# Ternary weights quantised by ScalarE in chunks during the first attention, in place of a stage of their own

## What is computed

```
x = x + _L0_xattn_ref(_layernorm(x), ctx_2048, Wq, Wkv, Wout, bout)
x = x + _L0_ffn_ref(_layernorm(x), w_gate, w_up, w_down)
...
def weight_quant(w):
    scale = 1.0 / jnp.clip(jnp.mean(jnp.abs(w)), EPS)
    return jnp.clip(jnp.round(w * scale), -1.0, 1.0) / scale
def bitlinear(x, w):
    return jnp.einsum('bsh,oh->bso', act_quant(x), weight_quant(w))
```

## Time and profile before

| | us |
|---|---|
| median of 3 runs | 2633.72 (2631.86 to 2634.31) |
| the profiled execution | 2634.14 |
| its span, first to last instruction | 2632.3 |
| mean granted clock of TensorE | 0.901 of full speed |

### The profile page before, as it was taken

One profiled execution on the slowest core, in us unless ns is written; L12 is line 12 of the kernel. 1 busy time (PEld: TensorE's weight loads), 2 busy tenths in 40 slices (PEclk: granted clock), 3 DMA queues, 4 the chain that ended last, 5 costly groups with the idle time before them and its releaser, 6 DMA issues. The chain is left out here.

```text
span 2632.3 us, 35153 instructions
## 1 busy us (share of the span) xinstructions
PE 2052.2 (78%) x11638; PEld 758.9 (29%) x11670; DVE 1586.2 (60%) x2348; ACT 1160.3 (44%) x1639; POOL 1314.3 (50%) x885
## 2 busy tenths in 40 slices
PE   4999999999999116999858898888944109999980
PEld 1222222222222002444322222222213105555540
DVE  5555555555553577776557777777725805565657
ACT  3555555555554014554324666666643004444420
POOL 2667666666767003766432222222212756777750
PEclk8999999999999558999978999999975559999995
DMA  2001010010101535000013323222201026666647
GB/s 93 22 22 34 22 30 27 29 30 22 34 18 34 200 104 168 1 1 1 0 43 53 59 58 58 54 55 52 45 29 48 1 59 174 202 188 209 193 129 320
DMA packets 166277, 192.37 MB, mean 73 GB/s; under 512 B 51014, under 2 KB 123206, under 8 KB 162928
## 3 DMA queue, kind: packets, MB, share of 16 engines
q1 hardware_dynamic: 143008, 151.38, 20.8%
q0 software_dynamic: 17408, 33.67, 3.9%
q10 hardware_dynamic: 5712, 5.45, 0.6%
HBM read 146.97 MB, written 59.93 MB: 79 GB/s over the span
## 5 line engine op out<-in xcount | busy, mean ns | idle before, releaser
L588 DVE TENSOR_REDUCE a_negmax<-a_ps_max 128x2 f32<-128x1024 f32 x256 | 312.1, 1219 | 226.7 <-PE a_ps_max L429 226.7
L1061 DVE TENSOR_REDUCE a_negmax<-a_ps_max 128x1 f32<-128x512 f32 x512 | 333.2, 683 | 119.5 <-PE a_ps_max L909 116.3
L1008 ACT ACTIVATE a_probs<-a_ps_st 128x512 f32<-128x512 f32 x512 | 288.9, 596 | 197.6 <-PE a_ps_st L930 195.2
L542 ACT ACTIVATE a_probs<-a_ps_st 128x1024 f32<-128x1024 f32 x256 | 262.0, 1024 | 232.2 <-PE a_ps_st L449 232.2
L389 POOL TENSOR_TENSOR a_added_up<-a_added_up,a_probs 128x1024 f32<-128x1024 f32 x128 | 301.0, 2352 | 29.8 <-ACT a_probs L542 27.2
L460 PE MATMUL a_ps_o<-a_probs,a_values 128*64 128x512 f32 x1024 | 276.2, 618 | 0.0
L389 POOL TENSOR_TENSOR a_added_up<-a_probs 128x1024 f32<-128x1024 f32 x64 | 150.2, 2347 | 227.8 <-ACT a_probs L542 227.8
L909 PE MATMUL a_ps_max<-a_k_st,a_q_st 96*128 96x512 f16 x512 | 201.6, 395 | 9.8 <-DVE a_negmax L1061 6.8
L930 PE MATMUL a_ps_st<-a_q_st,a_k_st 97*128 97x512 f16 x512 | 196.7, 386 | 8.3 <-ACT a_probs L1008 2.5
L43 PE MATMUL s_gu<-s_xT,s_gu_h 128*128 128x384 f16 x768 | 189.2, 329 | 1.9 <-DVE s_xT L2177 1.9
L581 DVE SCALAR_TENSOR_TENSOR a_qk_l<-a_ps_misc,a_qk_h 128x512 f16<-128x512 f32 x122 | 84.3, 691 | 137.3 <-ACT a_qk_h L525 137.3
(11 more groups left out here) (414 smaller groups left out, 4261.9 us busy)
## 6 DMA issues: line engine op xcount, KB each, us to landing
s_raw<-in_guT SPq DMA_DIRECT2D x32, 768.0 KB, 5.7
a_inverse<-a_dram_inverse SPq DMA_DIRECT2D x128, 128.0 KB, 3.0
m_y_tok<-f_nothing SPq DMA_DIRECT2D x16, 1024.0 KB, 10.3
c_yg<-m_y_tok SPq DMA_DIRECT2D x16, 1024.0 KB, 7.8
a_ctx_in<-in_ctx SPq DMA_DIRECT2D x32, 256.0 KB, 3.0
s_raw<-in_dnT SPq DMA_DIRECT2D x32, 256.0 KB, 6.0
s_raw<-in_dnT SPq DMA_DIRECT2D x64, 128.0 KB, 6.8
a_q_st<-a_dram_halves SPq DMA_DIRECT2D x48, 128.0 KB, 3.7
```

The source lines that it names most:

```text
L542: act.activation(probs[:, s % RING, :, :], ps_st[:, :, :], ACT.Exp).then_inc(exped, 1)
L588: dve.tensor_reduce(negmax[:, v % 2, :, i % KD], ps_max[:, :, :], AX.X, ALU.max, negate=True).then_inc(maxed, 1)
L1008: act.activation(probs[:, s // HG % 3, s % HG, :], ps_st[:, s % 2, :], ACT.Exp, scale=DH1 ** -0.5).then_inc(exped, 1)
L1061: dve.tensor_reduce(negmax[:, g % 2, at:at + 1], ps_max[:, i % 2, :], AX.X, ALU.max, negate=True).then_inc(maxed, 1)
```

## The change

The quantisation stage is removed. `wq` and `means` become tensors of the whole kernel's first half, and the weights go through 96 chunk turns of the first attention, each 128x512 f32 (256 KB). There are 48 chunks, 16 for each weight, and each is loaded twice.

- First pass, chunks m = 0 to 47 in the even steps 16 to 110: ACT takes the absolute value with a sum over the row into `w_part` (the values it writes into `wq` are overwritten in the second pass).
- At step 114 DVE sums `w_part`; PE multiplies with ones at the end of step 118; at the end of step 119 PE waits for DVE, which makes means and reciprocals.
- Second pass, m = 48 to 95 in the even steps 128 to 222: ACT scales the chunk and adds 12582912, which rounds it, in place; in the odd step after it, it takes the sign of the chunk minus 12582912 and writes the ternary weight into `wq`.
- SP loads each chunk six steps ahead of its turn. There are three slots; the load of m waits until chunk m - 3 has been used, which the first pass signals with its one instruction and the second with the sign.
- The probabilities have 5 buffers for 6, the sums 3 pairs for 4, and queries and keys 7 pairs of heads for 8. The waits that guard these buffers are changed to match. Two constants are set by DVE before the attention, and `ones` has 128 columns for 32.

The rest of the kernel is as before. The diff, cut to its core:

```diff
-def first_attention(nc, x_all, stats, mv, rstd, d):
+def first_attention(nc, x_all, stats, mv, rstd, wq, means, d):
...
-    RING = 6
+    RING = 5
+    CHUNKS = 3 * KD * FF // D
+    PER = CHUNKS // 3
+    SLOTS = 3
+    UPS = 3
+    QK = 7
+    SUMMED_FROM, ROUNDED_FROM = STEPS, 8 * STEPS
+    MEANS_AT = 7 * STEPS + 2
...
-        ones = sb("ones", [P, P // HG], F32)
-        qk_h, qk_l = sb("qk_h", [P, 2, 2 * KD, D], F16), sb("qk_l", [P, 2, 2 * KD, D], F16)
+        ones = sb("ones", [P, P], F32)
+        magic = sb("magic", [P, 2], F32)
+        w_raw = sb("w_raw", [P, SLOTS, D], F32)
+        w_part = sb("w_part", [P, CHUNKS], F32)
+        w_sums = sb("w_sums", [P, 3], F32)
+        w_inv = sb("w_inv", [P, 3], F32)
+        qk_h, qk_l = sb("qk_h", [P, QK, 2, D], F16), sb("qk_l", [P, QK, 2, D], F16)
...
-        added_up = sb("added_up", [P, 2, HG, D], F32)
+        added_up = sb("added_up", [P, UPS, 2, D], F32)
...
+        def chunk_at(s):
+
+            if SUMMED_FROM <= s < SUMMED_FROM + 2 * CHUNKS and s % 2 == 0:
+                return (s - SUMMED_FROM) // 2
+            if ROUNDED_FROM <= s < ROUNDED_FROM + 2 * CHUNKS and s % 2 == 0:
+                return CHUNKS + (s - ROUNDED_FROM) // 2
+            return None
...
+            def load_chunk(m):
+                need(sp, w_used, m - SLOTS + 1)
+                w, c = m % CHUNKS // PER, m % PER
+                src = d[("wgT", "wuT", "wdT")[w]]
+                cols = src.shape[1] // D
+                sp.dma_start(w_raw[:, m % SLOTS, :], src[P * (c // cols):P * (c // cols) + P, D * (c % cols):D * (c % cols) + D]).then_inc(w_in[m % SLOTS], 16)
+
             load_context(1)
             place_maxima(0)
             load_context(2)
             for s in range(T):
                 g = s // 8 - 1
+                if chunk_at(s + 6) is not None:
+                    load_chunk(chunk_at(s + 6))
                 if s % KD == 2 and s // KD + 1 < KD * B:
                     place_maxima(s // KD + 1)
...
+            def total_weights():
+                pe.wait_ge(w_step, 1)
+                pe.wait_ge(maxrow, MEANS_AT // KD + 3)
+                need(pe, sums_kept, MEANS_AT // 8)
+                nc.tensor.matmul(ps_tr[:, 0:3], ones[:, :], w_sums[:, :], start=True, stop=True).then_inc(w_total, 1)
...
+                if s == MEANS_AT + 4:
+                    total_weights()
+                if s == MEANS_AT + 5:
+                    pe.wait_ge(w_step, 3)
...
+            def chunk(m):
+                w, c = m % CHUNKS // PER, m % PER
+                raw_w, out_w = w_raw[:, m % SLOTS, :], wq[:, w, D * c:D * c + D]
+                act.wait_ge(w_in[m % SLOTS], 16 * (m // SLOTS + 1))
+                if m < CHUNKS:
+                    act.activation(out_w, raw_w, ACT.Abs, accum_out=w_part[:, m:m + 1]).then_inc(w_used, 1)
+                else:
+                    act.wait_ge(w_step, 3)
+                    act.activation(raw_w, raw_w, ACT.Identity, bias=magic[:, 0:1], scale=w_inv[:, w:w + 1]).then_inc(w_rounded, 1)
+
+            def chunk_sign(m):
+                w, c = m % CHUNKS // PER, m % PER
+                act.wait_ge(w_rounded, m - CHUNKS + 1)
+                act.activation(wq[:, w, D * c:D * c + D], w_raw[:, m % SLOTS, :], ACT.Sign, bias=magic[:, 1:2], scale=1.0).then_inc(w_used, 1)
...
+                if chunk_at(s) is not None:
+                    chunk(chunk_at(s))
+                if s > ROUNDED_FROM and chunk_at(s - 1) is not None:
+                    chunk_sign(chunk_at(s - 1))
...
+            def weight_sums():
+                dve.wait_ge(w_used, CHUNKS)
+                dve.tensor_reduce(w_sums[:, :], w_part[:, :].rearrange("p (w c) -> p w c", w=3), AX.X, ALU.add).then_inc(w_step, 1)
+
+            def weight_means():
+                dve.wait_ge(w_total, 1)
+                dve.tensor_scalar(means[:, :], ps_tr[:, 0:3], 1.0 / (D * FF), Q_EPS, ALU.mult, ALU.max).then_inc(w_step, 1)
+                dve.wait_ge(w_step, 2)
+                dve.reciprocal(w_inv[:, :], means[:, :]).then_inc(w_step, 1)
...
+                if s == MEANS_AT:
+                    weight_sums()
+                if s == MEANS_AT + 5:
+                    weight_means()
...
-def quantise_weights(nc, wq, means, d):
...
-def ternary_ffn(nc, x_all, stats, mv, rstd, ident, d, y_tok):
+def ternary_ffn(nc, x_all, stats, mv, rstd, wq, means, ident, d, y_tok):
...
-        wq = sb("wq", [P, 3, KD * FF], BF16)
-        means = sb("means", [P, 3], F32)
-        quantise_weights(nc, wq, means, d)
```

More of the change, by code:

```diff
@@ L293, in first_attention @@
                  "weighted kept added summed sums_kept sums_out compact_in recip inverse_out inverse_in normalised out_proj residual").split())
+        w_in = [sem(f"w_in{q}") for q in range(SLOTS)]
+        w_used, w_rounded, w_step, w_total = (sem(n) for n in ("w_used", "w_rounded", "w_step", "w_total"))
         def first_context(sp):
@@ L302, in first_attention @@
             first_context,
-            [(row[:, :, :].bitcast(U32), 0, 0), (shift[:, :], WS, 0)], [(ones[:, :], 1.0, 0)], stats, mv, rstd[:, :, 0], (d["x"], x_all))
+            [(row[:, :, :].bitcast(U32), 0, 0), (shift[:, :], WS, 0)], [(ones[:, :], 1.0, 0), (magic[:, 0:1], MAGIC, 0), (magic[:, 1:2], -MAGIC, 0)], stats, mv, rstd[:, :, 0], (d["x"], x_all))
         block = ctx.enter_context(nc.Block())
@@ L312, in tile_left, with chunk_used_at @@
             need(eng, v_out, KD * n + max(t - 7, 0))
+        def chunk_used_at(m):
+            return SUMMED_FROM + 2 * m if m < CHUNKS else ROUNDED_FROM + 2 * (m - CHUNKS)
+        def chunk_at(s):
[4 more added lines that the diff above has]
+            return None
         def added_by(s):
@@ L366, in _ @@
             sp.wait_ge(rows_in, 32 * KD * B)
+            for q in range(SLOTS):
+                sp.wait_ge(w_in[q], 16 * 2 * CHUNKS // SLOTS)
             sp.wait_ge(inverse_in, 16 * HG * GROUPS)
@@ L381, in add_up @@
                 pool.wait_ge(exped, s + 1)
-                total = added_up[:, v // 2 % 2, 2 * (v % 2):2 * (v % 2) + 2, :]
+                total = added_up[:, v % UPS, :, :]
                 if j == 1:
-                    need(pool, summed, v // 2 - 1)
+                    need(pool, summed, (v - UPS) // 2 + 1)
                     first = probs[:, (s - 1) % RING, :, :]
@@ L428, in max_products @@
                 for half, rows in enumerate(HALVES):
-                    last = nc.tensor.matmul(ps_max[:, half, :], qk_h[rows, n % 2, 2 * u, P * t:P * t + P], qk_h[rows, n % 2, 2 * u + 1, :],
+                    last = nc.tensor.matmul(ps_max[:, half, :], qk_h[rows, i // KD % QK, 0, P * t:P * t + P], qk_h[rows, i // KD % QK, 1, :],
                                             start=True, stop=True)
@@ L444, in score_products @@
                     pe.wait_ge(lows, 8 * n + 2 * u + 2)
[L445 to L446 removed]
+                q_h, q_l = qk_h[:, v % QK, 0, :], qk_l[:, v % QK, 0, :]
+                k_h, k_l = (a[:, v % QK, 1, P * j:P * j + P] for a in (qk_h, qk_l))
                 for m, (a, b) in enumerate(((k_h, q_h), (k_l, q_h), (k_h, q_l), (shift[:, :], row[:, v % ROWS, :]))):
@@ L469, in sum_up @@
                     at = P // HG * hh
-                    last = nc.tensor.matmul(ps_tr[at:at + P // HG, :], ones[:, :], added_up[:, g % 2, hh, :], start=True, stop=True)
+                    last = nc.tensor.matmul(ps_tr[at:at + P // HG, :], ones[:, 0:P // HG], added_up[:, (2 * g + hh // 2) % UPS, hh % 2, :], start=True, stop=True)
                 last.then_inc(summed, 1)
@@ L523, in evacuate @@
                 if t < 8:
-                    need(act, scores, STEPS * (n - 1))
-                    act.activation(qk_h[:, n % 2, t, :], bank, ACT.Copy, scale=1 / WS).then_inc(evac_high, 1)
+                    v = KD * n + t // 2
+                    need(act, scores, KD * (v - QK + 1))
+                    act.activation(qk_h[:, v % QK, t % 2, :], bank, ACT.Copy, scale=1 / WS).then_inc(evac_high, 1)
                 else:
@@ L579, in low @@
                 dve.wait_ge(evac_high, 8 * n + t + 1)
-                need(dve, scores, STEPS * (n - 1))
-                dve.scalar_tensor_tensor(qk_l[:, n % 2, t, :], bank, 1 / WS, qk_h[:, n % 2, t, :], ALU.mult, ALU.subtract).then_inc(lows, 1)
+                v = KD * n + t // 2
+                need(dve, scores, KD * (v - QK + 1))
+                dve.scalar_tensor_tensor(qk_l[:, v % QK, t % 2, :], bank, 1 / WS, qk_h[:, v % QK, t % 2, :], ALU.mult, ALU.subtract).then_inc(lows, 1)
             def maxima(i):
@@ L2454, in build @@
         rstd3 = rstd[:, :].unsqueeze(2)
-        first_attention(nc, x_all, stats, mv, rstd3, d)
-        layer_norm_scales(nc, "ln1_", stats, mv, rstd)
-        ternary_ffn(nc, x_all, stats, mv, rstd3, ident, d, y_tok)
+        with nc.sbuf_tensor("wq", [P, 3, KD * FF], BF16) as wq, nc.sbuf_tensor("means", [P, 3], F32) as means:
+            first_attention(nc, x_all, stats, mv, rstd3, wq, means, d)
```

(2 more changed lines are left out.)

## The result

| | us |
|---|---|
| before, median of 4 runs | 2633.0 (2631.9 to 2634.3) |
| changed, median of 4 runs | 2692.1 (2686.2 to 2694.8) |
| ratio | 1.022, 95% interval 1.0208 to 1.0232 |
| the profiled execution | 2686.2, span 2684.2 |

The account below looks back on a forecast made before the run. PE was taken to bound the attention, with nothing running beside the quantisation stage. 2634.1 - 84.2 + 70.2 (second-pass stalls) + 9.4 (first pass) + 1.5 (means) + 30 (clock) = 2661 us, 1.0% slower; range 2628 to 2690.

Parts of the forecast that it names:

- The stage removed, 84.2 us: Between layer norm and ternary network: nothing ran beside the quantisation stage, so all 84.2 us are saved.
- ScalarE delays nothing: In the attention, ACT's chunk instructions, 0.72 us each, end within the 2.95 us step; cover 0.5 us, cost nothing.
- SP's wait decides: Second pass: SP waits for the sign with the rows queued behind; 22 PE stalls, 70.2 us; first pass 9.4 us.
- the 22 places and their three kinds: Second-pass stalls before score matmuls: six of 4.1 us, eleven of 3.1, five of 2.3.
- the forecast's covered case: Rival: rows land before PE needs them, so only the means cost; 2551 us, chance 0.05.
- The chain of 4.1 us: Second pass, step 6 of eight: evacuation and sign 1.43, chunk issue 0.58, rows' issue 1.22, landing 0.91; PE stands 4.1 us.
- The clock, 30 us: Behind second-pass pauses PE falls to half clock, 2 us each: all of 4.1, two in three of 3.1, one in three of 2.3.
- The means, 1.5 us: Between the passes, one matmul and PE's wait for DVE cost 1.5 us, between 0.5 and 4.
- The rival of the held clock: Same second-pass stalls, but PE stays at full speed: 2631 us, no slower than before; chance 0.12.
- The point of decision: A total loss of 84.2 us cancels the saving; with stalls of 81, falls of 3 us decide the sign.
- The table loads: Rival: the sign needs another ACT table, two loads of 1.28 us for each of 48 signs; 2720 us, chance 0.04.
- The Trainium skill's rule for a transfer: About 2 us fixed cost per transfer: each stall about 0.5 us longer, the sum some 14 us higher.

Follow-up runs that it names:

- Undoing the order alone: Changed kernel with the chunk load, still six steps ahead, put behind the step's other transfers, the rows among them: 2550.4 us, ratio 0.968.
- the sign in the same step: Changed kernel with ACT's sign right behind the rounding in its step, instead of one step later: 2607.2 us, ratio 0.990.
- the pauses filled: Changed kernel with 18, 14 or 10 pairs of overwritten matmuls ahead of PE's wait for the rows in the second pass's stalling steps: 2646.5 us, ratio 1.005.
- the rows first: Changed kernel where SP waits for the slot at the same place, but issues the rows before the chunk's load: 2648.3 us, ratio 1.006.

## Why the prediction was right in kind and too small

The direction, the place and the mechanism were as forecast: 2661 us was said and 2692.1 measured, a rise of 59 us for 27, and 2.1 us above the stated range of 2628 to 2690. The spreads that the forecast gives its terms add up to 2630 and 2693 (2661 less 6 and 25, and with 9, 20 and 3), not to its 2634 and 2690. Two terms of the sum were too small, the chain and the clock. By its steps:

- **The stage removed, 84.2 us.** Right: 83.7.
- **ScalarE delays nothing.** Right, at prices near the 0.72 us taken (0.81, 0.71, and 0.82 for the absolute value), and with more cover than counted; see the sign in the same step.
- **SP's wait decides.** Right, with the 22 places and their three kinds. Undoing the order alone gives 2550.4, where the forecast's covered case said 2551.
- **The chain of 4.1 us.** The first term that was mis-sized. For step 136 three links differ: the sign ends 1.31 us in, not 1.43, the chunk's issue costs 0.45 us, not 0.58, and PE starts 1.76 us after the rows' issue instead of 0.91. I had taken the landing from the sums' transfers, which have nothing ahead of them; with nothing ahead of the rows it is 1.10. Behind w_down's loads, where it is 1.1 as well, the eight pauses came out as forecast, 26.0 us for 25.2; the error is in the 14 behind w_gate's and w_up's, 53.6 for 45.0. The bound of 0.4 us longer was too small for a pause of 4.75 against 4.14, and the sentence that 96 loads cost "nothing" had an exception: the transfer issued right behind one of w_gate or w_up. This is +9.4 us in the second pass and +8.0 in the first, where 0.2 us became about 0.8 in seven of the eleven places.
- **The clock, 30 us.** The second mis-sized term, +13.6. The price of a fall was right: 43.6 us over 21 falls is 2.1 each, and 2 was taken. The count was not. I gave the pauses of 3.1 us two in three and those of 2.3 one in three; they were mostly 3.7 and 2.85, and the clock fell behind 10 of 11 and 5 of 5. The longer chain is not the reason for all of it: the eight pauses behind w_down's loads had the lengths forecast, 2.3, 3.2 and 4.1 to 4.5 us, and the clock fell behind 8 of 8, where the forecast's chances give 5.3. The chances themselves were too low.
- **The means, 1.5 us.** 0.14 in place, and 0.7 in the start of the attention in this execution; too small to matter.
- **The rival of the held clock** lost in the changed kernel. With the pauses filled, the clock held and the kernel came to 2646.5, not 2631, which is still slower than before by 0.5%. The point of decision, 84 us of loss, was crossed by the pauses alone (97 us with the first pass).
- **The table loads.** None stands beside the signs; the attention's ACT work rises only by the chunks.
- **The Trainium skill's rule for a transfer** (DMA: Bandwidth & Descriptors, Anatomy of one DMA: some 2 us of fixed cost) would by the estimate have put the sum at 2675, nearer to the result. From the second row's issue to PE's start it is 0.6 + 1.1 = 1.7 us with nothing ahead, less than the Trainium skill's figure, and 0.6 + 1.76 = 2.4 behind a load of w_gate. The nearness is of the sum only: the rows show a cost that depends on what is ahead.

What stays open: why the rows land some 0.6 us late behind a load of w_gate or w_up and not behind one of w_down. Neither the layout of the source nor the order of the weights was varied.

## What to carry to other kernels

Work that moves into another stage brings its transfers along, and in a queue that is served in order the transfer that waits must stand behind those that someone needs soon: the same load, moved behind the step's four other kinds of transfer, turned 2.2% slower into 3.2% faster. Before a buffer ring is filled six steps ahead, count when its slot is given back; where that is after the step in which the load stands, the issuing engine stops there, with all that stands behind. And a pause of PE costs more than its length where the work behind it runs at half clock: here 43.6 us on top of 79.6.

## What the runs showed of the hardware

- Behind pauses of PE in dense work the clock fell to 1.2 GHz this often, in the second pass of the changed kernel, of the one with the rows first and of the one with the sign in the same step: pauses of 4.1 to 4.8 us, 6 of 6; 3.2 to 3.8 us, 16 of 17; 2.7 to 2.9 us, 12 of 14; 2.2 to 2.6 us, 7 of 8; up to 1.8 us, 0 of 21. Pauses shorter than the 3.6 us of the earlier trace rows thus did it too. In the changed kernel a fall took 2.1 us on average.
- Matmuls whose results nobody needs kept the clock at 1.00, and took 43.6 and 27.0 us of half clock out of two kernels.
- PE could start 1.1 us after the end of the rows' issue with no load ahead of them, and 1.6 to 1.8 us after it when a load of 256 KB in pieces of 2 KB, 8 KB apart, had been issued 0.45 us ahead. When that load was one block of 256 KB, it was 1.1 to 1.2 us.
